# Layer 3 of a four-layer kernel: patches loaded in one transfer of 128 partitions, planes laid out in DRAM by half, row and channel

## What is computed

```
def _L3_conv_ref(x, w, b):
    ...
    xp = (x with 3 mirrored pixels on every side)
    out = conv_general_dilated(xp, w, window_strides=(1, 1), padding='VALID', feature_group_count=192)
    return out + b[None, :, None, None]

x = x + _L0_conv_ref(_gn(x), ...)
x = x + _L1_conv_ref(_gn(x), ...)
x = x + _L2_conv_ref(_gn(x), ...)
x = x + _L3_conv_ref(_gn(x), L3_conv_w, L3_conv_b)
```

## Time and profile before

| | us |
|---|---|
| median of 3 runs | 2520.53 (2518.78 to 2528.45) |
| the profiled execution | 2517.25 |
| its span in the trace | 2515.5 |
| TensorE busy, all layers | 1945.1 (77%) |
| layer 3, from the first loads of its norm to the end | 2307.9 to 2515.5 |

### The profile page before, as it was taken

How to read it: one execution, slowest core, us unless ns; L and a number is a source line. 1 busy time by engine, 2 the same in 40 slices (tenths; PEclk the granted TensorE clock), 3 DMA queues, 4 the chain that set the end, 5 groups by cost and what they waited for, 6 DMA issues and landing times. The chain is left out here.

```text
span 2515.5 us, 36893 instructions
## 1 busy us (share of the span) xinstructions
PE 1945.1 (77%) x15660; PEld 1203.3 (48%) x15660; DVE 1287.4 (51%) x1313; ACT 804.7 (32%) x1269; POOL 870.2 (35%) x459
## 2 busy tenths in 40 slices
PE   3879779769999999999978768777777777774052
PEld 1577666667777777777734322222222222221031
DVE  6445444441111111111271166799999999988803
ACT  3445445440000000000122125633543533335410
POOL 3334233220000000000000040599899899983300
PEclk9889899889999999999988778899899979987555
DMA  7899999988131313130120040678688868863799
GB/s 197 249 311 314 316 292 304 296 257 241 59 118 59 118 60 118 60 118 1 43 59 11 0 139 21 156 197 219 171 213 216 209 175 213 218 179 90 224 215 294
DMA packets 195538, 424.51 MB, mean 169 GB/s; under 512 B 18733, under 2 KB 143661, under 8 KB 184717
## 3 DMA queue, kind: packets, MB, share of 16 engines
q1 hardware_dynamic: 182540, 414.81, 58.8%
q10 hardware_dynamic: 12832, 7.34, 1.1%
HBM read 299.33 MB, written 121.96 MB: 167 GB/s over the span
## 5 line engine op out<-in xcount | busy, mean ns | idle before, releaser
L743 PE MATMUL ps<-mem 128*128 128x288 f16 x5376 | 654.6, 287 | 14.4 <-DMA mem<-depthwise_out 14.4
L743 PEld LDWEIGHTS ps<-mem 128*128 128x128 f16 x5376 | 502.1, 98 | 152.9 <-issue 15.4
L1717 POOL TENSOR_TENSOR mem<-mem 128x1024 f32<-128x1024 f32 x192 | 465.7, 2444 | 45.3 <-ACT mem L1651 42.9
L1626 PE MATMUL ps<-mem 128*128 128x512 f32 x768 | 417.9, 676 | 39.1 <-POOL mem L1717 35.0
L1112 POOL TENSOR_TENSOR mem<-mem 128x1536 f16<-128x1536 f32 x16 | 50.8, 3180 | 940.3 <-ACT mem L1090 940.3
L533 PE MATMUL ps<-mem 56*96 56x240 f16 (+1 forms) x5184 | 308.2, 280 | 86.1 <-DMA mem<-base_phases 53.0
L533 PEld LDWEIGHTS ps<-mem 56*96 56x96 f16 x5184 | 297.7, 128 | 111.4 <-DMA mem<-base_phases 58.5
L786 DVE TENSOR_TENSOR mem<-ps,mem 128x128 f16<-128x128 f32 x64 | 18.7, 292 | 586.8 <-ACT mem L807 586.8
L1746 DVE TENSOR_TENSOR_SCAN mem<-mem,ps 128x1024 f32<-128x1024 f32 x132 | 307.8, 2332 | 18.2 <-issue 10.3
L646 DVE TENSOR_TENSOR mem<-ps,mem 96x1024 f16<-96x1024 f32 x144 | 175.3, 1220 | 217.9 <-ACT mem L578 217.9
L1626 PEld LDWEIGHTS ps<-mem 128*128 128x128 f32 x768 | 153.5, 213 | 242.9 <-issue 134.5
(11 more groups left out here) (202 smaller groups left out, 1915.4 us busy)
## 6 DMA issues: line engine op xcount, KB each, us to landing
mem<-l_bc SPq DMA_DIRECT2D x504, 256.0 KB, 4.5
depthwise_out<-mem SPq DMA_DIRECT2D x105, 512.0 KB, 9.4
mem<-depthwise_out SPq DMA_DIRECT2D x31, 1664.0 KB, 10.8
mem<-base_phases SPq DMA_DIRECT2D x72, 448.0 KB
base_phases<-mem SPq DMA_DIRECT2D x56, 512.0 KB, 9.9
mem<-in_wd SPq DMA_DIRECT2D x72, 336.0 KB
mem<-l_planes SPq DMA_DIRECT2D x48, 252.0 KB
mem<-in_x SPq DMA_DIRECT2D x4, 2048.0 KB, 13.6
```

The lines of the kernel that those rows point to most:

```text
L743: ins = nc.tensor.matmul(ps[:, 2 * (i % 2) + h, 0:HALF], d, pw[rows, wa, k, HALF * h:HALF * h + HALF], start=(k == 0 and n == 0), stop=(k ...
L1626: ins = nc.tensor.matmul(py[:, a, :], ident, hh[:, n % 4, 512 * a:512 * a + 512], start=(n % N == 0), stop=(n % N == N - 1))
L1717: nc.gpsimd.tensor_tensor(hh[:, n % 4, :], hh[:, n % 4, :], cs[:, n % 4, :], ALU.mult).then_inc(hc_pool, 1)
```

## The change

The change lies in layer 3, with one addition to layer 0.

- `planes_d` is laid out as [half, row, channel in half, image, 576 bytes], with 64 rows for each half instead of 56. A window of 128 partitions (64 rows of each half) by 8 channels by both images is then one DMA, in which each partition reads 9216 bytes in a piece. The 56 rows that count are written by the stores of layer 3. The other 8 are never used by a matmul, but are loaded; they are filled once at the start of the program, with zeros out of `ext`, by two DMAs of SP (`store_unused`), and POOL's first `shift` waits for these in place of `ext_cleared`.
- A tile's store is cut in two by channel: SP stores the first half of its channels, ACT the second. Each is written in runs of 576 bytes, 56 for a channel. For tiles 0 and 1 SP's half is partitions 0 to 63 and ACT's 64 to 127; for tile 2 each has two DMAs of 32 partitions.
- Windows 0 to 7 now pair channel c with channel c + 64, windows 8 to 11 channel 128 + c with 160 + c. So the weights are packed in another order, and the sums of a window go to `conv_d` in four DMAs instead of two.
- On SP the first three windows are issued ahead of tile 2's store, the others behind it.
- The low part of the taps is made by DVE in place of POOL: piece 0 after the rows of tile 0, pieces 1 and 2 after those of tile 1, and piece 3 in tile 2 ahead of its shifted phases. The taps are loaded with 128 partitions instead of 120.

```diff
-        planes_d = nc.dram_tensor("l3_planes", [B, C, TAPROWS, 2 * PLANE], F16).ap()
+        planes_d = nc.dram_tensor("l3_planes", [2, 64, C // 2, B, 2 * PLANE], F16).ap()
...
+    def store_unused(sp, t):
+
+        size = B * 2 * PLANE
+        src = ext[0:C // 2].rearrange("c s r n -> c (s r n)")[:, 0:(64 - TAPROWS) * size].rearrange("c (r n) -> c r n", n=size)
+        sp.dma_start(planes_d[t, TAPROWS:64].rearrange("r c b n -> c r (b n)"), src).then_inc(sem.unused_planes, 16)
...
+        sp.wait_ge(ext_cleared, 1)
+        for t in range(2):
+            store_unused(sp, t)
...
             split_taps(0)
-            pool.wait_ge(ext_cleared, 1)
+            pool.wait_ge(sem.unused_planes, 32)
...
+    def store_planes(eng, t, h):
+
+        for p0, b, c0, n in pieces(t):
+            lo = p0 + n // 2 * h
+            eng.dma_start(planes_d[h, 0:TAPROWS, c0 // 2:c0 // 2 + n // 2, b].rearrange("f c n -> c f n"),
+                          pl[lo:lo + n // 2, t % 2].rearrange("p c r h n -> p (c r) (h n)")).then_inc(stored[t], 16)
...
-            for t in range(NT):
-                if t < 2:
-                    sp.wait_ge(tap_hi, t + 1)
-                    sp.wait_ge(tap_lo, t + 1)
-                    load_taps(sp, t + 2)
+            def load_windows(n):
+                src = planes_d.rearrange("t f c b n -> (t f) c (b n)")[:, BP * n:BP * n + BP]
+                sp.dma_start(win[:, n % NW], src).then_inc(win_in[n % NW], 16)
+
+            for t in range(2):
                 sp.wait_ge(rows_done, t + 1)
-                for p0, b, c0, n in pieces(t):
-                    sp.dma_start(planes_d[b, c0:c0 + n].rearrange("c f n -> c (f n)"),
-                                 pl[p0:p0 + n, t % 2].rearrange("p c r h n -> p (c r h n)")).then_inc(stored[t], 16)
+                store_planes(sp, t, 0)
+                sp.wait_ge(tap_hi, t + 1)
+                sp.wait_ge(tap_lo, t + 1)
+                load_taps(sp, t + 2)
             sp.wait_ge(tap_hi, NPIECE)
             sp.wait_ge(tap_lo, NPIECE)
-            sp.wait_ge(stored[0], used + 16)
-            sp.wait_ge(stored[1], used + 16)
-            for n in range(NB3):
-                if n >= NW:
-                    sp.wait_ge(conv_sum, n - NW + 1)
+            sp.wait_ge(sem.unused_planes, 32)
+            sp.wait_ge(stored[0], used + 32)
+            sp.wait_ge(stored[1], used + 32)
+            for n in range(NW):
+                load_windows(n)
+            sp.wait_ge(rows_done, NT)
+            store_planes(sp, 2, 0)
+            for n in range(NW, NB3):
+                sp.wait_ge(conv_sum, n - NW + 1)
                 if CB * n == 128:
-                    sp.wait_ge(stored[2], used + 32)
-                for t in range(2):
-                    for b in range(B):
-                        c0 = CB * n + BP * t
-                        sp.dma_start(win[64 * t:64 * t + TAPROWS, n % NW, :, 2 * PLANE * b:2 * PLANE * b + 2 * PLANE],
-                                     planes_d[b, c0:c0 + BP].rearrange("c f n -> f c n")).then_inc(win_in[n % NW], 16)
+                    sp.wait_ge(stored[2], used + 64)
+                load_windows(n)
...
-            for t in range(NT):
-                shift_right(t)
-                if t + 1 < NT:
-                    normalise(t + 1)
-                taps(t + 1)
+            shift_right(0)
+            normalise(1)
+            store_second(0)
+            taps(1)
+            shift_right(1)
+            taps(2)
+            store_second(1)
+            normalise(2)
+            taps(3)
+            shift_right(2)
+            store_second(2)
...
+            def taps(i):
+                dve.wait_ge(tap_hi, i + 1)
+                s, q = slice(3 * WC * i, 3 * WC * (i + 1)), slice(0, 64 + TAPROWS)
+                V.tensor_tensor(wh[q, 1, s], w32[i % 2][q], wh[q, 0, s], ALU.subtract).then_inc(tap_lo, 1)
```

More of the change, by code:

```diff
@@ L160, in fresh @@
             return a
-        layer0_depthwise(nc, sem, fresh(), ps, inp, xin, ident, base_d, d_dram, gacc)
+        layer0_depthwise(nc, sem, fresh(), ps, inp, xin, ident, base_d, d_dram, gacc, planes_d)
         vpx = mem[:, SIZE - NT * HW:SIZE].bitcast(F16).rearrange("p (a f t c) -> p a f t c", a=2, f=PHASES, t=NT)
@@ L294, in group_norm, with layer0_depthwise @@
     return rs, nb
-def layer0_depthwise(nc, sem, ar, ps, inp, xin, ident, base_d, d_dram, spare):
+def layer0_depthwise(nc, sem, ar, ps, inp, xin, ident, base_d, d_dram, spare, planes_d):
     xn = ar.take(NT, HW)
@@ L326, in layer0_depthwise @@
     ext_cleared = sem("l0_shifted_cleared")
+    sem.unused_planes = sem("l3_unused_planes_stored")
     ext_done = sem("l0_base_shifted")
@@ L1900, in _ @@
-            sp.wait_ge(stored[2], used + 32)
+                sp.wait_ge(conv_stored[k], 64 * (128 // CB // NSTG))
+            sp.wait_ge(stored[2], used + 64)
             for t in range(NT):
@@ L1917, in _ @@
             for n in range(NB3):
-                pe.wait_ge(win_in[n % NW], win_base[n % NW] + 64 * (n // NW + 1))
+                pe.wait_ge(win_in[n % NW], win_base[n % NW] + 16 * (n // NW + 1))
                 if n == 0:
@@ L1967, in _ @@
                 for b in range(B):
[L1968 to L1974, removed]
-                s = slice(3 * WC * i, 3 * WC * (i + 1))
-                q = slice(0, 64 + TAPROWS)
-                nc.gpsimd.tensor_tensor(wh[q, 1, s], w32[i % 2][q], wh[q, 0, s], ALU.subtract).then_inc(tap_lo, 1)
-            for i in range(NPIECE):
-                taps(i)
+                    for t in range(2):
+                        dst = channels(conv_d, b, n)[t].rearrange("(h j) (f n) -> (j f) h n", j=4, f=M3)
+                        src = stg[:, n % NSTG, :].rearrange("p (t h b n) -> p t h b n", t=2, h=2, b=B)[:, t, :, b]
+                        act.dma_start(dst, src).then_inc(conv_stored[n % NSTG], 16)
         @block.vector
@@ L2005, in _ @@
                 if t == 2:
-                    dve.wait_ge(stored[0], used + 16)
+                    dve.wait_ge(stored[0], used + 32)
                 for r in range(4):
@@ L2012, in _ @@
                 dve.wait_ge(x_lo, 4 * t + 4)
+                if t == 2:
+                    taps(3)
                 V.tensor_copy(grid(pl[:, k, 11:14])[:, :, :, 0:7], grid(pl[:, k, 0:3])[:, :, :, 1:8]).then_inc(shifted, 1)
@@ L2017, in _ @@
                 rows(t)
+                for i in ((0,), (1, 2), ())[t]:
+                    taps(i)
             dve.wait_ge(bias_in, 16)
@@ L2093, in layouts @@
     o["sel2"] = sel.reshape(96, -1)
-    w3 = v["L3_conv_w"][:, 0].reshape(C // (2 * BP), 2, BP, 7, 7)
-    wd3 = np.zeros((64 + TAPROWS, C // (2 * BP), BP, YS, PHASES), f)
+    w3 = v["L3_conv_w"][:, 0]
+    w3 = np.concatenate([w3[0:128].reshape(2, 8, BP, 7, 7).swapaxes(0, 1), w3[128:192].reshape(2, 4, BP, 7, 7).swapaxes(0, 1)], 0)
+    wd3 = np.zeros((128, C // (2 * BP), BP, YS, PHASES), f)
     for n, (s, p, r) in enumerate(rows):
```

16 lines of the change are left out of this document (11 added, 5 removed).

## The result

| | before | after |
|---|---|---|
| median, us (20 runs each) | 2520.89 (2511.9 to 2528.45) | 2503.11 (2490.04 to 2517.35) |
| profiled execution | 2517.25 | 2508.77 |
| its span | 2515.5 | 2506.9 |
| layer 3, start of its first load to the end of the span | 207.6 | 192.6 |

The ratio is 0.9932, 95% interval 0.9919 to 0.9944: 0.7% faster, clear of the scatter, and by under half of what was forecast (2479, range 2455 to 2506). Inside layer 3 the profile shows 15.0 us less. The layer started at 2314.28 instead of 2307.89 in the two profiled executions. So I compare times counted from the start of layer 3, and set 6.4 us against each time of after to compare it with the forecast's clock.

The account below looks back on a forecast made before the run. Layer 3's first half was taken as bound by a DVE and ACT chain, its second by DMA. Window 3 at 2400, 38.7 us for nine windows and the tail gave a 2474 span, 2479 against the median; range 2455 to 2506.

Parts of the forecast that it names:

- The first half: Layer 3 up to window issue: rows of tiles 0 and 1 complete at 2330.8 and 2345.1, windows issued at 2373.
- The first half gains nothing: Layer 3 before the windows: stores take the place of POOL's stalls, so windows issue at 2373 against 2374 before.
- T = 19: Stores of planes in layer 3: one tile's store takes 19 us, between readings of 20.4 and 17.2.
- the halves take turns: Stores of planes: DMAs on the two partition halves do not overlap, so two queues buy nothing; stores at some 217 GB/s.
- Rival 1: Stores of planes: the halves overlap, a tile's store takes 12.9 us, 16 us less, time 2463; chance 0.2.
- Window 3 at 2400: Layer 3's second half: window 3 lands at 2400 behind tile 2's store, so TensorE starves from about 2390.
- Nine windows at 4.3 us: TensorE's last nine windows: 4.3 us each, 38.7 us in all, so TensorE ends at 2439 instead of 2481.6.
- The tail, 34.9: From TensorE's end to the span's end: 33.9 us as before plus 1 for two more DMA issues.
- ACT's issue of its first half: ACT's store of its half of tile 0: issued at 2338, after its four normalisations.
- Costed at nothing: Start of the program: two stores of zeros, 1.77 MB, some 6 us, hidden by the start of layer 0.
- Of the rivals, 2: Stores of planes: short runs cost stores what they cost loads, 26.5 us a tile, time 2500; chance 0.2.
- rival 3: Window loads: one transfer no faster than four, 6.6 us a window, 21 us more, time 2500; chance 0.07.

Follow-up runs that it names:

- run 3: Kernel before, with only the taps' low parts moved from POOL to DVE: median 2507.4 us, ratio 0.9952 to before.
- run 4: Changed kernel, but SP issues both halves of each tile's store and ACT stores no planes: median 2523.7 us, ratio 1.0001 to before.
- run 5: Changed kernel, but ACT stores its two pieces of tile 2 in swapped order (the swap): median 2495.3 us, ratio 0.9882 to before.
- run 8: Changed kernel, but windows 3 to 11 are not loaded and reuse data of windows 0 to 2: 2494.6 us, executed once.
- run 2: Changed kernel, but the zeros are stored at the start of layer 3 instead of in layer 0: median 2504.0 us, ratio 0.9928 to before.
- run 10: Changed kernel with ACT's tile 2 pieces swapped and third and fourth tap loads issued ahead of stores: median 2492.3 us, ratio 0.9883 to before.

## Why the prediction missed, by its own steps

- **The first half** was right: the rows, DVE's low part (2.55 us for 2.7), no stretched DVE instruction, the landing of the fourth taps (2367.9 on the forecast's clock for 2368), and the issue of windows. That the taps landed on time is luck in part. The sum was 8.3 MB of planes at 217 GB/s, with no time for the two loads of taps, 2.4 MB. Measured, from 2338.6 to 2374.2, it was more bytes at a higher rate:

```profile
DMA packets 13775, 10.10 MB, mean 284 GB/s; under 512 B 80, under 2 KB 13519, under 8 KB 13519
```

"The first half gains nothing" is right as a sum; run 3 shows its two terms, 6.9 us gained and 5.6 spent.
- **T = 19, "the halves take turns": failed.** From the first issue to the last landing tile 0 took 25.1 us, tile 1 27.4 (they overlap), and tile 2 29.8. Tiles 0 and 1 were both in DRAM 3.2 us later than the forecast's 2369, which the taps hid. The reason was wrong too. The halves take turns in one queue (177 GB/s) and when both queues are on the same half (181), but not otherwise (293). The earlier trace rows were no test, since there SP moved 128 partitions and ACT 64. Rival 1's mechanism is real, but its T = 12.9 was reached by no tile: ACT's half of tile 0, issued at 2337.26, had moved only 0.08 MB in 2340 to 2343, and its half of tile 1 was issued 6.6 us late.
  The rule that I weighed, from the Trainium skill ("SBUF — State Buffer", Can I just issue two DMAs to hit both halves?), says 6% for two DMAs on the two halves. Here it is 66% for stores in 576-byte runs, and run 4, which goes back to one queue, has a layer 3 that is 14.8 us longer. On this kernel the measurement decides against it.
- **Window 3 at 2400: failed, 10.7 us late, 1.6 of them inherited.** The forecast gave tile 2 the same T as the others, 19 us; measured, its stores were issued on time (2376.5 on the forecast's clock) and landed 29.8 us later. Two things are in it. Its pieces put both queues on the same half; run 5 mends that, and window 3 comes 6.9 us earlier. And "windows 0 to 2 are loads and run beside it" gave 3.5 MB of loads no time. With the swap, window 3 is still 3.8 us later than forecast; that these loads are the reason was not tested.
- **Nine windows at 4.3 us: failed, and it is the largest miss, 12.7 us.** The step took TensorE's need as 4.04 us, the bare matmuls of the earlier trace rows at 1.2 GHz, and the DMA engines as the bound. It put the stops at nothing. The trace of before had them. From 2446 to 2479 the DMA engines were full, but TensorE waited 0.5 us for a window and stopped between its blocks. The stretch (columns as in the earlier trace rows), and two blocks of it:

```profile
2446.00:2479.00 33.00, 18.68 (x652) 13.42 (x644) 1.09 (x2) 5.06 (x5) 0.00 (x0) 0.50 1.01 286
```

```profile
2467.13 3.61 PE L1931 MATMUL ps<-mem 56*32 56x256 f16 x127 [2.99 <-issue]
2473.33 3.61 PE L1931 MATMUL ps<-mem 56*32 56x256 f16 x128 [2.59 <-issue]
```

From 2449.64 to 2479.26 there are five blocks, 5.9 us apart, and that is 6.7 us a window. So the 6.6 us that the prediction read as the price of a window's transfer was also TensorE's own pace, stops included. After the change the clock is higher (granted 0.73 instead of the 0.52 of the earlier trace rows; blocks take 1.94 us at 2.4 GHz against 3.6 at 1.2), and TensorE waits for no window, but the eight blocks from 2423.97 to 2467.17 are 5.4 us apart. With quieter DMA engines they are 3.7 to 4.0 us apart at either clock (runs 8 and 2), which makes at least 4.2 us a window, and 5.7 was measured. Taking all window loads away (run 8) brings the nine windows to 47.1 us, not to 38.7. What made it more is the longer stops, which come beside busy DMA engines; that those cause them is likely from run 8 (1.8 us quiet, 5.1 and 5.7 busy), but no run shows how.
- **The tail, 34.9: measured 38.5 and, on the same code, 35.3.** No more can be read. ACT's issue of four stores per window was named as a way to be wrong ("if each window waited for its sums' four stores"); ACT does wait 54.4 us for its own issues, but TensorE didn't wait for it.
- **ACT's issue of its first half** was put at 2338, after four normalisations. It came at once with SP's, at 2337.26 (2330.9 on the forecast's clock), with three normalisations still to run.
- **Costed at nothing**: the zeros, confirmed by run 2.

Of the rivals, 2 gave near the measured time (2500) for a cause that isn't there: short runs cost the stores an eighth, 202 to 177 GB/s, and TensorE started at 2379, not 2392. The same holds for rival 3, also 2500: one transfer is faster, and yet the windows came slowly. So it is luck that the range, which reached out for these two, holds the measured 2503.

## What to carry to other kernels

When a load becomes faster, price the engine that consumes it by how far apart its blocks of work start in a stretch where it waits for no load, and not by its bare work. When two queues share a transfer of SBUF, see that at each moment one is on partitions 0 to 63 and the other on 64 to 127 (293 GB/s here, against 181), and put small loads that a chain waits for ahead of big stores. Before crediting a change with its result, run each part of it alone: here moving the taps' low parts to DVE had 12.5 of the 15.0 us of layer 3.

## What the hardware showed that I had not expected

- Two queues storing from different halves of SBUF moved 293 to 301 GB/s, on the same half 181, one queue alone 165 to 177.
- In layer 3 TensorE stops after 128 matmuls and their weight loads, at times after 256. With DMA engines about half busy the blocks of 128 start 3.74 to 4.02 us apart at 2.4 GHz (run 8) and once 3.85 at 1.2 GHz (run 2); beside busy ones, in the changed kernel, up to 7.0 us.
- ACT issued a DMA while activations written ahead of it were still to run: at 2337.26, with the next of three starting at 2337.82.
- An engine that issues a DMA behind big stores can stand still in it: SP 6.5 and 9.6 us at the loads of taps (0.33 us ahead of the stores, run 10), ACT up to 21.3 us at the four stores of a window's sums.
